# Expert bias in a buffer of its own, x_raw in one slot, and expert-weight loads issued one batch per step

## The reference

```python
# layer 0: a weight matrix chosen per batch entry
x = x + einsum('bsd,bdh->bsh', x, W0[cat_ids]) + b0[cat_ids]
# layer 1: a shared MLP, whose last 128 output columns come from a chosen expert
h      = gelu(x @ fc1_w.T + fc1_b)                     # hidden size 2048
shared = h @ fc2_w.T + fc2_b                           # 384 columns
expert = einsum('bnh,bph->bnp', h, experts_w[idx]) + experts_b[idx]   # 128 columns
x = x + concatenate([shared, expert], -1)
```

## Time and profile before

| | us |
|---|---|
| median of 3 runs | 1796.58 (1796.12 to 1799.9) |
| the profiled execution | 1797.1 |
| its span (first to last instruction) | 1795.3 |
| PE busy | 1692.8 (94%) |
| DVE busy | 1168.7 (65%) |
| ACT busy | 547.4 (30%) |
| POOL busy | 213.7 (12%) |

### The profile page before, as it was taken

How to read it: one execution, slowest core, us unless ns; L and a number is a source line. 1 busy time by engine, 2 the same in 40 slices (tenths; PEclk the granted TensorE clock), 3 DMA queues, 4 the chain that set the end, 5 groups by cost and what they waited for, 6 DMA issues and landing times.

```text
span 1795.3 us, 27887 instructions
## 1 busy us (share of the span) xinstructions
PE 1692.8 (94%) x7297; PEld 1362.8 (76%) x7297; DVE 1168.7 (65%) x1944; ACT 547.4 (30%) x927; POOL 213.7 (12%) x198
## 2 busy tenths in 40 slices
PE   6899898998989989899898989989899898998999
PEld 4687687887878878788787878878788786887887
DVE  5677566676666766666666666756667666666665
ACT  4333232232323323233232332322333232332221
POOL 1110202002020020200201011020200202002010
PEclk9899999999999999999999999999999999999999
DMA  8756546455464554555555464554645545555330
GB/s 246 157 135 148 114 103 145 96 127 110 104 150 94 132 113 106 130 111 131 109 114 116 105 146 102 128 114 105 151 93 131 114 106 133 106 128 118 78 69 24
DMA packets 750034, 212.99 MB, mean 119 GB/s; under 512 B 676069, under 2 KB 690549, under 8 KB 749941
## 3 DMA queue, kind: packets, MB, share of 16 engines
q1 hardware_dynamic: 749508, 211.35, 52.7%
q10 hardware_dynamic: 432, 0.79, 0.1%
HBM read 195.24 MB, written 16.78 MB: 118 GB/s over the span
## 4 chain that ended last, share of the span: by engine, by line
PE 69%; SPq 11%; DVE 8%; issue 5%; DMA 4%; POOL 1%; ACT 1%; DVEq 1%; ACTq 0%
PE ps_out L715 31%; PE ps_h L700 15%; PE ps_e L700 13%; PE ps_y L687 8%; SPq L319 6%; DMA resid<-in_L_cond_experts_b 3%; DVE resid L578 2%; SPq L290 2%; SPq L329 1%; PE ps_t L641 1%; DVE h L510 1%; DVE x_whole_t L525 1%; DVE w_split L510 1%; DMA w_raw<-in_L_cond_W 1%; DVE x_t L510 1%
## 5 line engine op out<-in xcount | busy, mean ns | idle before, releaser
L715 PE MATMUL ps_out<-w2e,h 128*128 128x512 f32 x3072 | 776.4, 401 | 0.0
L715 PEld LDWEIGHTS ps_out<-w2e,h 128*128 128x128 f32 x3072 | 587.9, 192 | 142.4
L700 PE MATMUL ps_e<-y_t,w 128*128 128x512 f32 x1536 | 381.0, 398 | 1.4 <-DVE y_t L510 1.4
L700 PE MATMUL ps_h<-y_t,w 128*128 128x512 f32 x1536 | 377.8, 396 | 0.0
L700 PEld LDWEIGHTS ps_e<-y_t,w 128*128 128x128 f32 x1536 | 291.1, 190 | 71.1 <-DVE y_t L510 1.8
L700 PEld LDWEIGHTS ps_h<-y_t,w 128*128 128x128 f32 x1536 | 289.4, 188 | 68.3
L687 PE MATMUL ps_y<-w_split,x_t 128*128 128x512 f32 x744 | 227.3, 416 | 79.0 <-DVE x_t L510 74.2
L450 ACT CAST w2e<-e_whole 128x512 fp32r<-128x512 f32 x256 | 158.9, 621 | 439.4 <-PE ps_out L715 439.4
L566 DVE CAST h<-g_raw 128x512 fp32r<-128x512 f32 x256 | 111.9, 437 | 250.7 <-ACT g_raw L462 248.8
L687 PEld LDWEIGHTS ps_y<-w_split,x_t 128*128 128x128 f32 x744 | 143.1, 197 | 115.0 <-DVE w_split L510 72.5
L559 DVE CAST w2e<-w2e 128x512 fp32r<-128x512 f32 x256 | 123.1, 481 | 156.5 <-PE ps_out L715 156.3
(11 more groups left out here) (51 smaller groups left out, 453.8 us busy)
## 6 DMA issues: line engine op xcount, KB each, us to landing
w_raw<-in_L_cond_W SPq DMA_DIRECT2D x256, 256.0 KB, 2.8
e_blocks<-in_L_cond_experts_w SPq DMA_DIRECT2D x1024, 64.0 KB, 2.5
b_all<-in_L_cond_b SPq DMA_DIRECT2D x64, 256.0 KB, 3.4
out<-resid SPq DMA_DIRECT2D x64, 256.0 KB, 2.2
x_blocks<-in_x SPq DMA_DIRECT2D x240, 64.0 KB, 2.4
x_raw<-in_x SPq DMA_DIRECT2D x60, 256.0 KB, 3.1
prep_raw<-in_L_cond_fc_w SPq DMA_DIRECT2D x22, 256.0 KB, 3.4
resid<-in_L_cond_experts_b SPq DMA_DIRECT2D x64, 64.0 KB, 2.8
```

The lines of the kernel that those rows point to most:

```text
L700: last = nc.tensor.matmul(h_bank(c)[:, :], w1[:, w, k, c * P:(c + 1) * P], y_t[:, a, k, :, :].rearrange("p b s -> p (b s)"), start=(k == 0 ...
L715: last = nc.tensor.matmul(ps_out[b][:, :], h[:, c % 2, a, b * S:(b + 1) * S], fc2_columns(c, c % 2, w, b), start=(c == 0 and n == 0), stop ...
```

## The change

Six things are edited. (1) The expert bias goes to a buffer of its own, `be_all`; it is loaded a group ahead (in step 15 of the group before) and waits only for that group's `add_out_bias`. (2) `x_raw` has one slot instead of two: `load_x` waits for `y_sum` of the batch entry before, and is issued in the third step of a quad. (3) `load_experts` is called in every step, for one batch entry (4 transfers), where it was called in the second and third step for two each (8 transfers). So its first call of a quad is now in the quad's first step, ahead of `store` and of `load_l0`. (4) `turn_x` on DVE goes from the end of a quad's last step to the end of its third. (5) In the start-up part, the first 16 expert transfers and the first expert bias are issued after `load_l0(1, 0, 0)`, not before layer 0's last two weight loads. (6) `y_low(0, 3)` goes ahead of `turn_e(0, 0)`.

```diff
@@ load_x
-                after(sp, y_ready, G * GB + b - 1)
-                sp.dma_start(x_raw[:, b % 2, :], x[bass.ds(G * GB + b, 1), :, :].rearrange("o s d -> (o s) d"))\
-                  .then_inc(x_in[b % 2], 16)
+                after(sp, y_ready, G * GB + b)
+                sp.dma_start(x_raw[:, :], x[bass.ds(G * GB + b, 1), :, :].rearrange("o s d -> (o s) d"))\
+                  .then_inc(x_in, 16)
@@ load_l0
-                if k == 1 and not first(G):
+                if k == 2 and not first(G):
                     load_x(G, b)
@@ load_expert_bias
-                if first(g):
-                    sp.wait_ge(x_turned, GB)
-                    sp.wait_ge(xb_ready, GB)
-                after(sp, out_stored, g * GB * 16)
+                after(sp, resid_ready, g * GB)
                 for b in range(GB):
-                    sp.dma_start(resid[:, b, SHARED:D], exp_b[bass.ds(idx[b], 1), :].to_broadcast([P, PART]))\
+                    sp.dma_start(be_all[:, b, :], exp_b[bass.ds(idx[b], 1), :].to_broadcast([P, PART]))\
                       .then_inc(be_in, 16)
@@ SP, start-up and body(g, more)
-                if j == NC - 2:
-                    load_experts(0, 0, first_experts, range(GB))
...
+            load_l0(1, 0, 0)
+            load_experts(0, 0, first_experts, range(GB))
+            load_expert_bias(0, first_experts)
...
                 for c in range(NC):
-                    if c % QUAD in (1, 2):
-                        batches = range(2) if c % QUAD == 1 else range(2, GB)
-                        if c + QUAD < NC:
-                            load_experts(g, c // QUAD + 1, idx, batches)
-                        elif more:
-                            next_idx = {b: index(exps, (g + 1) * GB + b, exp_w.shape[0]) for b in batches}
-                            load_experts(g + 1, 0, next_idx, batches)
+                    batches = [c % QUAD]
+                    if c + QUAD < NC:
+                        load_experts(g, c // QUAD + 1, idx, batches)
+                    elif more:
+                        if c % QUAD == 0:
+                            next_idx = [index(exps, (g + 1) * GB + b, exp_w.shape[0]) for b in range(GB)]
+                        load_experts(g + 1, 0, next_idx, batches)
+                    if more and c == NC - 1:
+                        load_expert_bias(g + 1, next_idx)
                     load_prep(sp, prep_in_step(g, c))
                     if c == WSLOTS and not first(g):
                         store(g - 1)
-                    if c == (2 if first(g) else WSLOTS + 1):
-                        load_expert_bias(g, idx)
-                    if more:
+                    if more and not (first(g) and c == 0):
                         load_l0(g + 1, c // KD, c % KD)
@@ POOL, add_out_bias
-                nc.gpsimd.tensor_tensor(resid[:, b, SHARED:D], y[:, b, SHARED:D], resid[:, b, SHARED:D], ALU.add)\
+                nc.gpsimd.tensor_tensor(resid[:, b, SHARED:D], y[:, b, SHARED:D], be_all[:, b, :], ALU.add)\
@@ DVE
-            turn_e(0, 0)
             y_low(0, GB - 1)
+            turn_e(0, 0)
...
                     h_low(g, c)
-                    if more and c % KD == KD - 1 and c + 1 < NC:
+                    if more and c % KD == KD - 2 and c + 2 < NC:
                         turn_x(g + 1, c // KD + 1)
```

More of the change, by code:

```diff
@@ L78, in build @@
         w_split = sb("w_split", [P, 2, 2, D], F32R)
-        x_raw = sb("x_raw", [P, 2, D])
+        x_raw = sb("x_raw", [P, D])
         x_blocks = sb("x_blocks", [P, D])
@@ L93, in build @@
         b1_rows = e_blocks[0:NC, 1, 0, 0:P]
+        be_all = sb("be_all", [P, GB, PART])
         resid = sb("resid", [P, GB, D])
@@ L108, in build @@
         x_blocks_in = sem("x_blocks_in")
-        x_in = [sem(f"x_in{i}") for i in range(2)]
+        x_in = sem("x_in")
         first_x_in = [sem(f"first_x_in{b}") for b in range(GB)]
@@ L396, in add_b0 @@
                     pool.wait_ge(first_x_in[b], 16)
-                    after(pool, y_ready, b - 1)
+                    after(pool, y_ready, b)
                     source = resid[:, b, :]
                 else:
-                    after(pool, x_in[b % 2], 16 * ((G - 1) * (GB // 2) + b // 2 + 1))
-                    source = x_raw[:, b % 2, :]
+                    after(pool, x_in, 16 * ((G - 1) * GB + b + 1))
+                    source = x_raw[:, :]
                 after(pool, b0_in, 16 * (G * GB + b + 1))
-                nc.gpsimd.tensor_tensor(x_raw[:, b % 2, :], source, b0_all[:, :], ALU.add).then_inc(xb_ready, 1)
+                nc.gpsimd.tensor_tensor(x_raw[:, :], source, b0_all[:, :], ALU.add).then_inc(xb_ready, 1)
             def add_out_bias(G, b):
@@ L408, in add_out_bias @@
                 after(pool, out_stored, G * GB * 16)
+                if first(G) and b == 0:
+                    pool.wait_ge(x_turned, GB)
                 if b == 0:
@@ L538, in y_sum @@
                 after(dve, resid_ready, (G - 1) * GB + b + 1)
-                nc.vector.tensor_tensor(y[:, b, :], l0_bank(G, b)[:, :], x_raw[:, b % 2, :], ALU.add).then_inc(y_ready, 1)
+                nc.vector.tensor_tensor(y[:, b, :], l0_bank(G, b)[:, :], x_raw[:, :], ALU.add).then_inc(y_ready, 1)
             def turn_e(g, c):
@@ L596, in _ @@
                     y_sum(0, j // KD)
+            y_low(0, GB - 1)
             turn_e(0, 0)
-            y_low(0, GB - 1)
             def body(g, more):
```

## The result

The changed kernel takes 1975.09 us (median of 4 runs, 1968.18 to 1982.51) beside 1796.98 us for the kernel before (four runs here, where the table ahead of the prediction had three). The ratio is 1.0989, with a 95% interval of 1.0947 to 1.1031: it is slower by 10%. The forecast was 1964 us, range 1905 to 2045. The profiled execution took 1982.51 us and its span is 1980.7 us, 185.4 us more than before; the mean granted TensorE clock fell from 0.968 to 0.944.

A forecast was written before the change was run, and what follows sets the result against it. PE, busy for 94% of the span, was the floor, so only its gaps could change. New stalls of +155.4 us in 14 groups, +11.7 in group 0 and 0 for start-up gave +167 on 1797.1: 1964 us, range 1905 to 2045.

The forecast's parts named there:

- The mechanism: Step 4q - 2: `turn_e`, SP's wait and issues, `x_blocks`, `turn_x`, `w_low`, `l0_slice` form one chain; PE waits three times a group.
- q = 1 term: PE before `l0_slice(3)`, with the stores in the chain: a 5.8 us wait, +0.5 over the old 5.3.
- The upper end of the earlier trace: Landing of `x_blocks` in the old kernel's profile: up to 3.4 us when expert transfers share queues; 2.4 was used.
- The half clock: PE matmuls run at 1.2 instead of 2.4 GHz right after idling: 1.7 us extra per 3.6 us gap.
- The rival without the half clock: A 3.6 us gap may be too short to lower PE's clock; 31 gaps lose 1.7 us: 1911 us, chance 0.10.
- the old stall: Step 4, 14 times: PE waits 5.3 us for `x_low` as `y_sum` awaits POOL; 7.4 us with the clock's 2.1.
- q = 2 and 3 in 14 groups: PE waits 3.6 us before `l0_slice` at each, plus 1.7 for clock: 5.3 each, 10.6 a group.
- three stalls of group 0: Group 0 gets three stalls, 15.9 us, less 4.2 for its existing gap: +11.7 us.
- the heavier rival: `x_blocks` land 1.0 us later in 45 places and clock costs 2.9 in 31: 2046 us, chance 0.09.
- The expert bias: Own buffer takes its load off the path to `y_sum`: worth 104 us in 14 groups if nothing replaced the stall.
- forecast for this case: Faster rival: `x_blocks` arrive before DVE stands still for long, 104 us are gained, 1693 us; chance 0.08.
- Start-up: PE's 9.92 us gap goes, but expert and bias transfers now precede the first step's: between -10 and +5, taken as 0.

The follow-up runs named there:

- load_l0 first: Changed kernel with a quad's first-step `load_experts` call moved behind the stores and `load_l0`: 1695.46 us, ratio 0.9402 to the kernel before.
- turn_x late: Changed kernel with only `turn_x` put back at the end of a quad's last step: 1742.21 us, ratio 0.9658 to the kernel before.
- stores one step later: Changed kernel with the four stores moved to step 5, behind the `x_blocks` of step 4: 1988.72 us, ratio 1.1031 to the kernel before.
- bias back in `resid`: Changed kernel with `load_experts` behind `load_l0` in a quad's first step, and the expert bias loaded into `resid` at step 5: 1789.29 us, ratio 0.9905.

## Why the prediction was right, step by step

**The mechanism** is the one foretold: wait, issues, `x_blocks`, `turn_x`, `w_low` closed within step 4q - 2. It is in the trace link by link, and moving only the wait's side (load_l0 first) or only `turn_x` takes away all or most of the loss.

**The gaps.** Forecast were 5.8, 3.6 and 3.6 us a group. The group shown has 6.56, 4.43 and 3.38. Over the run the 14 gaps at q = 1 lie between 6.14 and 6.82 us (mean 6.4), and the 31 others between 2.7 and 4.4 (mean 3.45). PE's idle time before this `l0_slice` rose from 79.0 to 203.8 us, 125 more, where the forecast's terms give 14 x 7.7 + 10.8 - 2.8 = 116.

```profile
L688 PE MATMUL ps_y<-w_split,x_t 128*128 128x512 f32 x744 | 235.5, 427 | 203.8 <-DVE w_split L511 203.5
```

The q = 1 term was too small, by 14 x 0.6 = 8.4 us. From the end of `turn_e(3)` to the first `x_blocks` issue the forecast has 6.4 us and the trace 936.07 - 929.08 = 7.0, since the stores' issues with their gaps took 2.3 and the category read started slower, 1.33 from its start to `x_blocks` instead of 0.94. The 4.43 has another source: after the last `x_blocks` issue of that quad the chain has 3.37 us of transfer and not 2.4. The upper end of the earlier trace rows is real, but such gaps, of over 4 us, are 2 of the 31. A further 0.3 us in step 1 of each group was not foreseen.

**The half clock** was priced at 1.7 us for a gap of 3.6 us. Behind the gap of 3.38 the `l0_slice` took 1.33 for 0.85 and `fc2` 4.19 for 2.96, 1.7 together; behind 4.43 it is 1.7, behind 6.56 it is 2.2. In the loop groups most gaps of 3.0 to 3.9 us cost 1.6 to 1.7, but five of them (of 3.06 to 3.48 us) cost 0.1, and one of 3.09 cost 2.7; group 0's first two, 3.62 and 3.84 us, cost 2.4 and 2.8 (an undisturbed `l0_slice` takes 0.95 there). The rival without the half clock, 1911 us, is refuted by these rows. PE's busy time rose by 58.5 us, where the forecast has 28 x 1.7 + 5.1 - 1.4 = 51, but not all of that is clock: the last matmul of a `fc1` is listed as overlapping the next row by 0.16 us (`fc1` 2.96 long, the next starts 2.80 later), a gap ends that overlap, and some 40 new gaps make 6 us of it.

**The sum.** 125 + 58.5 = 183.5 of the 185.4 us by which the span grew. The forecast was 167; between the medians it is 178. In the forecast's own terms, measured from the start of one `fc1` to the next beside the same step undisturbed (6.28 us in the loop groups), and within 2 us of the whole:

| term | forecast | measured |
|---|---|---|
| q = 1 in 14 groups, over the old stall | +7 | +20 |
| q = 2 and 3 in 14 groups | +148 | +141 |
| three stalls of group 0 | +16 | +18 |
| start-up, with the old gap of 2.77 us gone | -4 | +2 |
| step 1 in 14 groups | 0 | +6 |

Every step of the mechanism holds. The sizes of q = 1 (the gap by 0.6 us, clock and lost overlap 2.4 us for 2.1) and of the start-up were too small, and step 1 was not in the sum. The 28 stalls of q = 2 and 3 cost 0.3 us less each than forecast, which pays for part of this: that is luck. One slip in the range changes nothing: its lower end, 1905, takes 0.2 us of landing in 31 places, and in all 45, as the heavier rival counts them, it would be 1902.

**The expert bias.** That its wait goes, and that its gain is eaten up by the new stall at q = 1, was right: the version with load_l0 first has the gain (ratio 0.9402; forecast for this case 1693 us, measured 1695 beside 1803). That the gain is the bias buffer's is shown by the run with it put back: without the buffer 91 us are lost again.

**One `x_raw` slot** was costed at nothing. It is in the version that takes 1695 us with PE busy for 98%, so it costs little there; it was not tried by itself.

**Start-up** was taken as 0 between -10 and +5. It came out at +6, just outside. PE's gap of 9.92 us went, one of 10.45 us came in its place, and the old gap of 2.77 us went too (it stands at step 2 of group 0, not at step 3 as the prediction has it). Yet group 0's `fc1` of step 3 starts at 77.75 us where it started at 75.96, though 4.4 us of gap and half clock ahead of it are gone:

```profile
60.60 1.12 PE L642 MATMUL ps_t<-ident,prep_raw 128*128 128x128 f32 x4 [10.45 <-DMA prep_raw<-in_L_cond_fc_w]
```

**What was left out** is the second victim of the moved wait: the weights of step 4q. The prediction says that they land in time once DVE has stalled, which is so; but with `turn_x` late, where DVE hardly stalls, the late `load_l0` still cost 47 us. The rule of the Trainium skill (DMA: Bandwidth & Descriptors, Rules for kernel authors: issue early, wait late) had the sign right. The trace agrees: 333.8 us of DVE's waiting are exposed, of which PE feels 197.

## What to carry to other kernels

In an in-order issue queue a wait costs what stands behind it: before moving one up, list every transfer that it is moved past, and for each the time at which it is wanted. If the consumer of one of those transfers stands on the engine that the wait is for, and close behind the awaited instruction, the loop closes and its whole length shows. Here moving the wait back behind those transfers, with the same transfers, took the ratio from 1.0989 to 0.9402. Of the 6% below the kernel before, the buffer for the expert bias is 5% (0.9905 without it).

## What was unexpected of the hardware

The price of the half clock does not follow a gap's length, and for short gaps it comes out either way. A gap of 1.97 us (turn_x late, above) left `l0_slice` at 0.96 us and `fc2` at 2.96. One of 2.25 us (stores one step later) was followed by 1.64 and 3.79. In the traces of the changed kernel, of turn_x late and of stores one step later, gaps of 1.8 to 3.5 us were followed by 0.1 us of extra matmul time or by 1.6 to 1.7, rarely by something else, and both occur over that whole stretch: 0.1 behind a gap of 2.57 and of 3.50 us, 1.7 behind one of 1.83. With the bias back in `resid` it is another price again: four gaps of 3.27 to 3.40 us cost 2.6 to 2.9 each, more than most gaps of over 6 us in the changed kernel (1.9 to 2.8). Before an `l0_slice` behind the start-up part, no gap under 1.8 us cost more than 0.13. A stall of 2 us can thus take 2 us or 3.7. What decides between the prices was not found.

A plain elementwise instruction on VectorE took 1.83 us instead of 0.69 while GpSimd was adding, and this alone opened a gap on TensorE in step 1 of the changed kernel:

```profile
920.28 1.30 POOL L402 TENSOR_TENSOR x_raw<-x_raw,b_all 128x512 f32<-128x512 f32 x1 [28.59 <-DMA x_raw<-in_x]
920.30 1.83 DVE L511 TENSOR_TENSOR h<-g_raw,h 128x512 fp32r<-128x512 f32 x1
922.06 0.68 DVE L511 TENSOR_TENSOR w_split<-w_raw,w_split 128x512 fp32r<-128x512 f32 x1
...
922.79 0.97 PE L688 MATMUL ps_y<-w_split,x_t 128*128 128x512 f32 x3 [0.31 <-DVE w_split L511]
```

Over the whole trace none of the 211 `h_low` that ran while GpSimd was idle took over 0.69 us, and the 38 that overlapped a GpSimd instruction by over 0.4 us took 1.45 in the mean. The transposes of `e_blocks`, which have one input, stayed at 0.71 us in all 17 such overlaps. No run took GpSimd's work away, so this is a correlation in the trace and not a test.
